# Edge layers of a graph network: target rows stored in edge order and loaded by plain DMA, index copies moved from GpSimd to ScalarE

## The chip, the cores and the metric

The kernel runs on one core of one Trainium2 chip. The metric is the device time of one execution in microseconds (us). Of the kernel before, three executions are shown, with their median.

## What is computed

Four graph layers run one after another on 100,000 nodes of 160 features (64 scalars and 32 vectors of three) and 25,000 edges, each with a source node `src` and a target node `dst`; the edges are sorted by `dst`. After each layer the new features are `layernorm(x + layer(x))`. The change touches the first three layers, which have this form (the third has no `alpha`, and a fixed factor in place of the count):

```python
y = linear(x)[src]                       # rows of the source nodes
w = mlp(edge_attributes)                 # one weight row for each edge
m = products of w, y and the 4 edge harmonics
s = segment_sum(m, dst)                  # by target node
x = layernorm(x + self_linear(x) * a + factor * (s @ W_out))
```

A target node's row needs four things: its own old row, the rows of its edges' sources, the sum over its run of edges, and its attribute `a`. Nodes that are no target of any edge are computed in a phase of their own, which the change leaves alone.

## The kernel before

The program is a row of phases: weights, all nodes without edges (to about 5,120 us of the span), the edge index, the three edge layers (5,148 to about 9,335 us), and then the attention layer in three phases. Each layer reads the node table of the layer before (`rows0`, `table1`, `table2`: rows of 164 floats, being features, mean, attribute and variance) and scatters the changed rows into the next one.

`edges_layer` (line 1071) does one edge layer; `l` is 0, 1 or 2 for the first, second and third. Edges go by 250 (two tiles of 125 partitions, `J` = 2) in four lanes (`LANES`), each lane with its own buffers and two PSUM banks. 25 rounds of four lanes make 100 *lane steps* for a layer. The order in which each engine issues its work is fixed by a table, `order` (line 1092): each step has a due time within a lane's round, and `staggered` (line 54) shifts the lanes by `part` = 10.70 and sorts. So within one lane step an engine does early steps of one lane and late steps of others. Each engine runs its list strictly in that order, and waits on counting semaphores. What follows touches these:

- GpSimd (POOL): `copy_keys` (line 1156), `roots` (line 1165, the powers of minus one half for the two rows of an edge; second and third layer only), `gather_next` with `gather` (lines 1140 to 1147), `scatter` (lines 1182 to 1190). An indirect DMA takes its row numbers from a small tile at a fixed address, so `gather` first copies four columns of row numbers into `ends_now` (line 1140), waits for that copy, and then issues four indirect DMAs (line 1147): source rows and target rows of each of two tiles. `scatter` does the same with `into_now` (line 1182) and two indirect DMAs (line 1190).
- VectorE (DVE): `root_attr` (lines 1223 and 1225), `normalize` (1236 and 1238), `mask` (1054 to 1056, reads `key_now`), products and factors, the new rows (1322, 1329), their statistics up to `widen` (1350, counted as `widened`), and the combinations of the messages (1269 to 1275, counted as `combined3`).
- ScalarE (ACT): `keep_attr` (1376) copies the target's attribute from the gathered row; the other steps copy PSUM results and activate.
- TensorE (PE): transposes (1436, 1448, 1450), matmuls, twelve filler matmuls per lane step (127), and the segment sums with the self term (1064 to 1068, 1494, 1496).
- SyncE (SP): three plain loads for each lane step (1123 to 1127).

`roots` of a lane waits for the rows gathered, DVE's `root_attr` waits for `roots`, `gather_next` waits for `normalize` (the buffer is then free), and `scatter` waits for `widened` of an earlier lane.

## Time and profile before

| | |
|---|---|
| Median of 3 runs | 12570.89 us (12570.47 to 12591.11) |
| The profiled execution's own time | 12567.56 us |
| Its span in the profile | 12565.9 us |
| Busy: PE, DVE, ACT, POOL | 9604.8, 8166.7, 4467.0, 5987.3 us |
| Granted TensorE clock, mean | 0.838 |
| The three edge layers, start of GpSimd's first and last instruction | 5147.9 and 9331.4 us |

Busy times are sums over instructions; an engine at 70% of the span may still be the one that sets the pace of a phase, so the phases are read one by one. POOL's DMA issues are counted busy (about 1.2 us each). In a timeline, the number in brackets is how long the engine was idle before the instruction, and what released it.

### The profile page before, as it was taken

How to read it: one execution, taken by the hardware profiler on the slowest of the kernel's cores; microseconds unless marked ns; L12 is line 12 of the kernel's file. 1: busy time of each engine (PE TensorE's matmuls, PEld its weight loads, DVE VectorE, ACT ScalarE, POOL GpSimd, SP SyncE). 2: the span in 40 equal slices, each digit the busy share in tenths (PEclk: the TensorE clock that was granted, in tenths of full speed). 3: DMA queues.
4: the chain of work that ended last, by engine and by line, in shares of the span. 5: the costliest groups of instructions: out<-in, count | busy, mean ns of one | idle time of the engine just before them, and what ended most of it. 6: DMA issues, size and time to landing. Idle time of an engine off the chain costs nothing. (4 is left out here: it accounts for less than half of the span.)

```text
span 12565.9 us, 239341 instructions
## 1 busy us (share of the span) xinstructions
PE 9604.8 (76%) x58771; PEld 8632.2 (69%) x58771; DVE 8166.7 (65%) x40535; ACT 4467.0 (36%) x16207; POOL 5987.3 (48%) x8005
## 2 busy tenths in 40 slices
PE   6777777777777777788868877788868788875998
PEld 5666666666666666677757776677757777765888
DVE  4555555555555555677756666566658888877777
ACT  3555555555555555322212221222212222221222
POOL 2333333333333333577756665666654444442444
PEclk8888878888888777899977787777778888888999
DMA  2222222222222222222211111211111111111111
GB/s 61 79 77 77 79 79 77 79 78 77 80 78 78 77 78 77 56 55 55 54 41 43 43 44 38 44 43 43 42 36 39 39 39 40 39 40 40 54 54 48
DMA packets 919772, 722.88 MB, mean 58 GB/s; under 512 B 453930, under 2 KB 871439, under 8 KB 919329
## 3 DMA queue, kind: packets, MB, share of 16 engines
q1 hardware_dynamic: 721696, 522.17, 14.8%
q0 software_dynamic: 197632, 196.80, 6.5%
q14 instruction: 410, 3.35, 0.1%
q8 instruction: 34, 0.56, 0.0%
HBM read 363.73 MB, written 360.00 MB: 58 GB/s over the span
## 5 line engine op out<-in xcount | busy, mean ns | idle before, releaser
L127 PE MATMUL bank<-ident 128*128 128x128 f32 x10000 | 1592.0, 313 | 97.2 <-PEq L883 59.3
L127 PEld LDWEIGHTS bank<-ident 128*128 128x128 f32 x10000 | 1539.6, 229 | 160.2 <-issue 60.0
L749 ACT ACTIVATE nodes_x<-nodes_z 125x161 f32<-125x161 f32 x2400 | 1006.5, 422 | 1515.6 <-DVE nodes_z L673 1515.4
L795 PE MATMUL bank<-ident,nodes_z 125*65 125x125 f32 x1600 | 496.6, 328 | 1216.2 <-DVE nodes_z L673 1215.9
L1147 POOL DMA_INDIRECT edge_rows<-table,edge_ends_now x832 | 1030.7, 1239 | 395.4 <-POOL edge_ends_now L1140 203.1
L795 PEld LDWEIGHTS bank<-ident,nodes_z 125*65 125x65 f32 x1600 | 262.0, 164 | 1294.4 <-issue 1293.9
L673 DVE SCALAR_TENSOR_TENSOR nodes_z<-bank,nodes_z 125x162 f32<-125x162 f32 x2400 | 812.3, 380 | 475.5 <-PE bank L814 451.0
L814 PE MATMUL bank<-self_v,nodes_v_t 128*125 128x98 f32 x4800 | 1079.0, 310 | 0.0
L663 DVE TENSOR_REDUCE nodes_sum<-nodes_z 125x2 f32<-125x322 f32 x400 | 195.2, 488 | 1298.6 <-DMA nodes_z<-rows 1298.3
L1190 POOL DMA_INDIRECT table<-edge_new,edge_into_now x600 | 742.0, 1237 | 486.0 <-issue 442.4
L812 PE MATMUL bank<-self_s,nodes_s_t 128*125 128x65 f32 x4800 | 931.2, 280 | 15.9 <-DVE ffn_y L233 13.7
L812 PEld LDWEIGHTS bank<-self_s,nodes_s_t 128*125 128x125 f32 x4800 | 870.3, 218 | 82.4 <-issue 38.0
L612 POOL TENSOR_SCALAR nodes_z<-nodes_sum 125x2 f32<-125x2 f32 x400 | 88.2, 220 | 1638.9 <-DVE nodes_sum L663 1638.9
L814 PEld LDWEIGHTS bank<-self_v,nodes_v_t 128*125 128x125 f32 x4800 | 808.9, 212 | 0.0
L627 POOL TENSOR_SCALAR nodes_x<-nodes_z,nodes_factor,nodes_offset 125x161 f32<-125x161 f32 x800 | 377.4, 482 | 764.5 <-DVE nodes_offset L692 764.5
L1739 POOL DMA_INDIRECT att_edge_rows<-table,att_edge_ends_now x416 | 511.8, 1230 | 194.1 <-POOL att_edge_ends_now L1732 98.9
L1223 DVE SCALAR_TENSOR_TENSOR edge_root_a<-edge_root,edge_rows 125x2 f32<-125x2 f32 x200 | 32.4, 162 | 878.5 <-POOL edge_root L1165 878.5
L1147 POOL DMA_INDIRECT edge_rows<-rows,edge_ends_now x416 | 506.0, 1216 | 195.9 <-POOL edge_ends_now L1140 99.7
L1408 ACT ACTIVATE edge_sums<-bank 125x163 f32<-125x163 f32 x600 | 151.2, 304 | 1235.9 <-PE bank L1496 1235.9
L271 POOL TENSOR_TENSOR ffn_root<-ffn_wide,half 125x4 f32<-125x4 f32 x400 | 403.1, 1008 | 327.9 <-DVE ffn_wide L198 327.9
L1273 DVE SCALAR_TENSOR_TENSOR edge_msg<-bank,edge_y,edge_msg 125x65 f32<-125x65 f32 x1800 | 509.8, 283 | 32.0
L1448 PE MATMUL bank<-ident,edge_xs 125*65 125x125 f32 x600 | 175.6, 314 | 447.1 <-DVE edge_xd L1238 434.3
(495 smaller groups left out, 31982.5 us busy)
## 6 DMA issues: line engine op xcount, KB each, us to landing
table<-nodes_z SPq DMA_DIRECT2D x1200, 160.2 KB
nodes_z<-rows SPq DMA_DIRECT2D x400, 160.2 KB
out<-nodes_res SPq DMA_DIRECT2D x400, 156.2 KB
nodes_v_t<-x_t SPq DMA_DIRECT2D x400, 94.7 KB
edge_dst_row<-dst SPq DMA_DIRECT2D x300, 122.1 KB
dest_rows<-kept SPq DMA_DIRECT2D x100, 316.4 KB
nodes_s_t<-x_t SPq DMA_DIRECT2D x400, 63.5 KB
kept<-att_keep SPq DMA_DIRECT2D x100, 218.8 KB
```

Source lines behind the costliest of these rows:

```text
L127: pe.matmul(banks[2 * ((n + lead) % LANES) + odd][:, 0:128], w["ident"][:, :], w["ident"][:, :], start=True, stop=True)
L271: p.tensor_tensor(f["root"][:, n, :], f["wide"][:, n, :], f["w"]["half"][:, 0:2 * J], ALU.pow).then_inc(t["pool"][n], 1)
L627: ins = p.tensor_scalar(x3[:, k, :], z[:, 3, k, 0:X], factor3[:, k:k + 1], offset3[:, k:k + 1], ALU.mult, ALU.add)
L673: ins = v.scalar_tensor_tensor(z[:, l + 1, k, 0:A + 1], banks[2 + n % 2][0:P, o:o + A + 1], z[:, l, k, A:A + 1], z[:, l, k, 0:A + 1], ALU. ...
L749: ins = act.activation(x3[:, k, :], z[:, l + 1, k, 0:X], ACT.Square, bias=z[:, l + 1, k, MEAN:MEAN + 1], scale=-1.0, accum_out=total[:, l, ...
L795: pe.transpose(banks[n % 2][0:S + 1, j * P:(j + 1) * P], z[:, l, k, 0:VS], ident)
L812: pe.matmul(banks[2 + n % 2][0:P, o:o + VS], xs[:, n, c], w[f"self_s{l}"][:, :], start=True, stop=True)
L814: ins = pe.matmul(banks[2 + n % 2][0:P, o + MEAN:o + A + 1], xv[:, n, c], w[f"self_v{l}"][:, :], start=False, stop=True, skip_group_check= ...
L1147: p.indirect_dma_start(e["rows"][:, n, side, j, :], None, source, bass.IndirectOffsetOnAxis(ap=e["ends_now"][:, side, k:k + 1], axis=0)).t ...
L1190: p.indirect_dma_start(target, bass.IndirectOffsetOnAxis(ap=e["into_now"][:, k:k + 1], axis=0), e["new"][:, n, j, :], None, bounds_check=n ...
L1273: v.scalar_tensor_tensor(scalars, bank[0:P, o:o + 1 + S], y, scalars, ALU.mult, ALU.add)
L1739: p.indirect_dma_start(e["rows"][:, n, side, j, :], None, table, bass.IndirectOffsetOnAxis(ap=e["ends_now"][:, side, k:k + 1], axis=0)).th ...
```

## The change

In the first and second layer, SP additionally stores the 250 new rows of each lane step in edge order, in a new DRAM tensor `ordered1` or `ordered2` (line `store_new`). In the second and third layer, SP loads those rows of the layer before with a plain DMA (`load_dst`) into the place of the target rows, and POOL gathers the source rows only. (Only the last edge of a target's run has that target's complete row; it is the only one whose result is scattered.) In all three layers the copies of keys, scatter numbers and gather numbers go from POOL to ACT's first step, `keep_attr`, one round ahead for the gather numbers; POOL's own copy is done once per layer for the first round. All due times but `load_dst`'s move back by 4.0, so that order among the old steps stays the same around the cycle.

```diff
+    sides = 1 if l else 2
+    per_gather = 16 * J * sides
+    ordered_view = [None if x is None else x.rearrange("(t p) f -> p t f", p=P) for x in ordered]
...
-              pool=["keys", *["roots"] * (l > 0)])
+              pool=["roots"] * (l > 0))
...
-             ("scatter", 33.1)]
+             ("scatter", 33.1), ("store_new", 33.1)]
+    order = [("load_dst", 0.0)] + [(step, begin + early) for step, begin in order]
...
+            def load_dst(n, i):
+                sp.wait_ge(t["dve"][n], count_at(t, i, "dve", "normed"))
+                gate(sp, t)
+                sp.wait_ge(t["act"][n], count_at(t, i, "act", "attr_kept"))
+                gate(sp, t)
+                sp.dma_start(e["rows"][:, n, 1, :, :], ordered_view[l][:, bass.ds(i * T + J * n, J), :]
+                             ).then_inc(dst_loaded[n], 16)
+
+            def store_new(n, i):
+                sp.wait_ge(t["dve"][n], count_at(t, i + 1, "dve", "widened"))
+                gate(sp, t)
+                sp.dma_start(ordered_view[l + 1][:, bass.ds(i * T + J * n, J), :], e["new"][:, n, :, :]
+                             ).then_inc(new_stored[n], 16)
...
-                p.tensor_copy(e["ends_now"][:, :, own], index["ends"][:, :, bass.ds(i * T + J * n, J)]
-                              ).then_inc(index_copied[n], 1)
-                p.wait_ge(index_copied[n], copies)
-                gate(p, t)
                 for j in range(J):
-                    for side in range(2):
+                    for side in range(sides):
...
-            def copy_keys(n, i):
...
             def roots(n, i):
-                p.wait_ge(gathered[n], 64 * i + 64)
+                p.wait_ge(gathered[n], per_gather * i + per_gather)
+                gate(p, t)
+                p.wait_ge(dst_loaded[n], 16 * i + 16)
                 gate(p, t)
...
             def scatter(n, i):
-                p.wait_ge(scattered[n], 16 * J * i + 16)
-                gate(p, t)
-                own = slice(J * n, J * n + J)
-                p.tensor_copy(e["into_now"][:, own], index["into_i"][:, bass.ds(i * T + J * n, J)]
-                              ).then_inc(index_copied[n], 1)
-                p.wait_ge(index_copied[n], 2 * i + 3)
+                p.wait_ge(t["act"][n], count_at(t, i + 1, "act", "attr_kept"))
                 gate(p, t)
                 p.wait_ge(t["dve"][n], count_at(t, i + 1, "dve", "widened"))
...
             def mask(n, i):
-                v.wait_ge(t["pool"][n], count_at(t, i + 1, "pool", "keys"))
+                v.wait_ge(t["act"][n], count_at(t, i + 1, "act", "attr_kept"))
...
             def keep_attr(n, i):
-                act.wait_ge(gathered[n], 64 * i + 64)
+                act.wait_ge(gathered[n], per_gather * i + per_gather)
+                gate(act, t)
                 act.wait_ge(scattered[n], 16 * J * i + 16)
+                gate(act, t)
+                if l:
+                    act.wait_ge(dst_loaded[n], 16 * i + 16)
+                    gate(act, t)
+                if l < 2:
+                    act.wait_ge(new_stored[n], 16 * i + 16)
+                    gate(act, t)
+                act.wait_ge(t["dve"][n], count_at(t, i, "dve", "masked"))
+                gate(act, t)
+                own, now = slice(J * n, J * n + J), bass.ds(i * T + J * n, J)
+                act.activation(e["key_now"][:, :, own], index["keys"][:, :, now], ACT.Copy)
+                act.activation(e["into_now"][:, own], index["into_i"][:, now], ACT.Copy)
+                act.activation(e["ends_now"][:, :, own], index["ends"][:, :, bass.ds(i * T + T + J * n, J)], ACT.Copy)
                 one(act.activation(e["new"][:, n, :, A:A + 1], e["rows"][:, n, 1, :, A:A + 1], ACT.Copy), n)
```

The change in POOL's list, in the body of the third layer's loop, one lane step before (in the names, `edge_` is the edge phase's prefix; `ISA` and `REGISTER_ALU` rows are address and wait work of the sequencer):

```order
L1165 TENSOR_TENSOR edge_root<-edge_rows,half 125x4
L1140 ISA
L1140 COPY edge_ends_now<-edge_ends 125x2x2
L1147 DMA edge_rows<-table,edge_ends_now 125x164 x4
L1182 ISA
L1182 COPY edge_into_now<-into_i 125x2
L1190 DMA table<-edge_new,edge_into_now 100000x164 x2
L1156 ISA
L1156 COPY edge_key_now<-edge_keys 125x2x2
L1165 TENSOR_TENSOR edge_root<-edge_rows,half 125x4
```

Between one `roots` and the next stand three copies and six indirect DMAs. With the change, two lane steps at the same place in POOL's list:

```order
L1171 DMA edge_rows<-table,edge_ends_now 125x164 x2
L1203 DMA table<-edge_new,edge_into_now 100000x164 x2
L1183 TENSOR_TENSOR edge_root<-edge_rows,half 125x4
L1171 DMA edge_rows<-table,edge_ends_now 125x164 x2
L1203 DMA table<-edge_new,edge_into_now 100000x164 x2
L1183 TENSOR_TENSOR edge_root<-edge_rows,half 125x4
```

Two of four gathers and the three copies are gone; the cycle roots, gather, scatter, roots is the same as before.

SP's list with the change, one lane step in the loop of the second layer:

```order
L1150 DMA ordered<-edge_new 125x2x164
L1144 ISA
L1144 DMA edge_rows<-ordered 125x2x164
L1130 ISA
L1130 DMA edge_attrs<-edge_attr 125x2x16
L1132 ISA
L1132 DMA edge_y<-edge_attr 125x2x4
L1134 ISA
L1134 DMA edge_dst_row<-dst 125x250
```

The store of one step's new rows stands ahead of the loads of the next round of the same lane, so these loads now wait behind `widened`.

ACT's list with the change, around its first step, in the second layer:

```order
L1417 ACTIVATE edge_dv_t<-bank 97x250
L1402 ISA
L1402 ACTIVATE edge_key_now<-edge_keys 125x2x2
L1403 REGISTER_ALU
L1403 ACTIVATE edge_into_now<-into_i 125x2
L1404 ISA
L1404 ACTIVATE edge_ends_now<-edge_ends 125x2x2
L1405 ACTIVATE edge_new<-edge_rows 125x2
L1382 REGISTER_ALU
L1431 ACTIVATE edge_f<-bank 128x250
```

The step has kept its place between the copy of the turned target rows and that of `linear`; three copies and their address work are added ahead of it.

## Rows read from the trace of the kernel before

**Rows 1.** Windows: length, busy us of PE, PEld, DVE, ACT, POOL; clock, DMA share, GB/s
```profile
5500.00:6000.00 500.00, 431.98 (x2924) 369.06 (x2923) 372.09 (x1761) 148.56 (x531) 350.79 (x400) 1.00 0.24 55
6600.00:7600.00 1000.00, 818.75 (x4416) 723.72 (x4416) 663.05 (x3105) 219.13 (x759) 636.32 (x690) 0.80 0.19 43
8100.00:9100.00 1000.00, 817.42 (x4436) 718.90 (x4435) 622.14 (x2835) 221.39 (x760) 634.63 (x694) 0.79 0.19 43
```
**Rows 2.** Timeline of POOL in the second layer (start, duration, instruction, idle before)
```profile
7019.21 0.41 POOL L1140 COPY edge_ends_now<-edge_ends 125x4 int32 x1 [1.84 <-DVE edge_xd L1238]
7020.61 1.29 POOL L1147 DMA_INDIRECT edge_rows<-table,edge_ends_now  x1 [0.99 <-POOL edge_ends_now L1140]
...
7025.32 1.21 POOL L1147 DMA_INDIRECT edge_rows<-table,edge_ends_now  x1 [0.30 <-issue]
...
7027.88 1.23 POOL L1190 DMA_INDIRECT table<-edge_new,edge_into_now  x1 [1.15 <-issue]
...
7030.62 0.21 POOL L1156 COPY edge_key_now<-edge_keys 125x4 f32 x1
7030.77 1.06 POOL L1165 TENSOR_TENSOR edge_root<-edge_rows,half 125x4 f32<-125x4 f32 x1
```
**Rows 3.** Timeline of DVE in the same lane step
```profile
7017.40 0.16 DVE L1223 SCALAR_TENSOR_TENSOR edge_root_a<-edge_root,edge_rows 125x2 f32<-125x2 f32 x1 [3.84 <-POOL edge_root L1165]
...
7023.97 0.16 DVE L1350 TENSOR_SCALAR edge_new<-edge_moments 125x2 f32<-125x2 f32 x1
...
7027.24 0.25 DVE L1275 SCALAR_TENSOR_TENSOR edge_msg<-bank,edge_y,edge_msg 125x32 f32<-125x32 f32 x1
7031.87 0.16 DVE L1223 SCALAR_TENSOR_TENSOR edge_root_a<-edge_root,edge_rows 125x2 f32<-125x2 f32 x1 [4.37 <-POOL edge_root L1165]
```
**Rows 4.** Timeline of DVE and POOL at the first layer's end
```profile
6310.06 0.16 DVE L1350 TENSOR_SCALAR edge_new<-edge_moments 125x2 f32<-125x2 f32 x1
...
6311.22 1.19 POOL L1190 DMA_INDIRECT table<-edge_new,edge_into_now  x1 [5.91 <-DVE edge_new L1350]
```
**Rows 5.** Third layer: timeline of DVE; line 1190 in window 8100:9100 (count, ns, starts)
```profile
8593.55 0.16 DVE L1223 SCALAR_TENSOR_TENSOR edge_root_a<-edge_root,edge_rows 125x2 f32<-125x2 f32 x1 [3.33 <-POOL edge_root L1165]
...
8599.32 0.23 DVE L1350 TENSOR_SCALAR edge_new<-edge_moments 125x2 f32<-125x2 f32 x1
...
L1190 POOL DMA_INDIRECT table<-edge_new,edge_into_now x140: 1212/1226/1242, 8098.9 to 9096.4; - x140
```
**Rows 6.** First layer: timeline of POOL; waits of PE in 5150:6290 (total, times, longest)
```profile
5600.67 1.38 POOL L1190 DMA_INDIRECT table<-edge_new,edge_into_now  x1 [1.15 <-issue]
...
5612.06 1.32 POOL L1190 DMA_INDIRECT table<-edge_new,edge_into_now  x1 [1.21 <-issue]
...
PE bank L1064 <- DVE edge_msg L1275: 101.2, 94, 1.2
```
**Rows 7.** Timeline of PE in the second layer, a lane step at the full clock
```profile
7019.01 0.29 PE L1448 MATMUL bank<-ident,edge_xs 125*65 125x125 f32 x1 [0.25 <-DVE edge_xd L1238]
...
7027.79 0.51 PE L1064 MATMUL bank<-edge_msg,edge_same 125*125 125x163 f32 x2 [1.53 <-DVE edge_msg L1275]
...
7029.85 0.41 PE L1496 MATMUL bank<-self_v,edge_dv_t 97*125 97x97 f32 x2
```
**Rows 8.** Timeline of ACT, the step after its first step
```profile
7023.48 0.38 ACT L1402 ACTIVATE edge_f<-bank 128x250 f32<-128x250 f32 x1 [1.65 <-PE bank L1467]
```
**Rows 9.** Timeline: plain loads issued, and the instruction that waited for them
```profile
6347.19 0.45 SPq L1127 DMA_DIRECT2D edge_dst_row<-dst  x1
...
6352.22 0.58 PE L1436 MATMUL bank<-ident,edge_attrs 125*16 125x125 f32 x2 [7.39 <-DMA edge_dst_row<-dst]
...
3002.74 2.10 SPq L582 DMA_DIRECT2D nodes_z<-rows  x1
...
3012.16 0.49 DVE L663 TENSOR_REDUCE nodes_sum<-nodes_z 125x2 f32<-125x322 f32 x1 [4.01 <-DMA nodes_z<-rows]
```
**Rows 10.** DMA queues of the page: packets, MB, share of 16 engines
```profile
q1 hardware_dynamic: 721696, 522.17, 14.8%
```

More of the change, by code:

```diff
@@ L1107, in edges_layer @@
     scattered = [sem(f"edges{l}_rows_scattered_lane{n}") for n in range(LANES)]
-    index_copied = [sem(f"edges{l}_index_copied_lane{n}") for n in range(LANES)]
+    dst_loaded = [sem(f"edges{l}_dst_rows_loaded_lane{n}") for n in range(LANES)]
+    new_stored = [sem(f"edges{l}_new_rows_stored_lane{n}") for n in range(LANES)]
+    first_ends = sem(f"edges{l}_first_ends_copied")
     ready = sem(f"edges{l}_ready")
@@ L1129, in load, with gather @@
                              ).then_inc(attrs_loaded[n], 16)
-            run_rounds(sp, rounds, order, part, dict(load=load))
+            def load_dst(n, i):
[10 more added lines that the diff above has]
+                             ).then_inc(new_stored[n], 16)
+            for n in range(LANES):
+                sp.sem_inc(new_stored[n], 16)
+            run_rounds(sp, rounds, order, part, dict(load=load, **(dict(load_dst=load_dst) if l else {}),
+                                                     **(dict(store_new=store_new) if l < 2 else {})))
+            if l < 2:
+                for n in range(LANES):
+                    sp.wait_ge(new_stored[n], 16 * rounds + 16)
         @block.gpsimd
         def _(p):
-            prime(p, t, "pool")
-            def gather(n, i, copies):
-                own = slice(J * n, J * n + J)
-                p.tensor_copy(e["ends_now"][:, :, own], index["ends"][:, :, bass.ds(i * T + J * n, J)]
-                              ).then_inc(index_copied[n], 1)
-                p.wait_ge(index_copied[n], copies)
-                gate(p, t)
+            if l:
+                prime(p, t, "pool")
+            def gather(n):
                 for j in range(J):
-                    for side in range(2):
+                    for side in range(sides):
                         k = J * n + j
@@ L1149, in gather, with roots @@
                                              ).then_inc(gathered[n], 16)
-            def copy_keys(n, i):
-                p.wait_ge(t["dve"][n], count_at(t, i, "dve", "masked"))
+            def roots(n, i):
+                p.wait_ge(gathered[n], per_gather * i + per_gather)
                 gate(p, t)
-                own = slice(J * n, J * n + J)
-                p.tensor_copy(e["key_now"][:, :, own], index["keys"][:, :, bass.ds(i * T + J * n, J)]
-                              ).then_inc(t["pool"][n], 1)
-            def roots(n, i):
-                p.wait_ge(gathered[n], 64 * i + 64)
+                p.wait_ge(dst_loaded[n], 16 * i + 16)
                 gate(p, t)
@@ L1174, in gather_next @@
                 gate(p, t)
[L1175 removed]
+                gather(n)
             def scatter(n, i):
[L1179 to L1184 removed]
+                p.wait_ge(t["act"][n], count_at(t, i + 1, "act", "attr_kept"))
                 gate(p, t)
@@ L1192, in scatter @@
                                          ).then_inc(scattered[n], 16)
+            p.tensor_copy(e["ends_now"][:, :, :], index["ends"][:, :, 0:T]).then_inc(first_ends, 1)
+            p.wait_ge(first_ends, 1)
             for n in range(LANES):
                 p.dma_start(e["first"][:, n:n + 1], inp["node_vec1"][0:P, :]).then_inc(scattered[n], 16)
-                gather(n, 0, 1)
-            run_rounds(p, rounds, order, part, dict(copy_keys=copy_keys, **(dict(roots=roots) if l else {}),
-                                                    gather_next=gather_next, scatter=scatter))
+                gather(n)
+            run_rounds(p, rounds, order, part, dict(**(dict(roots=roots) if l else {}), gather_next=gather_next,
+                                                    scatter=scatter))
             for n in range(LANES):
-                p.wait_ge(gathered[n], 64 * (rounds + 1))
+                p.wait_ge(gathered[n], per_gather * (rounds + 1))
                 p.wait_ge(scattered[n], 16 * J * rounds + 16)
@@ L2534, in program @@
     tables = [inp["rows0"]] + [nc.dram_tensor(f"table{l}", (nodes, ROW), F32).ap() for l in range(1, 4)]
+    ordered = [None] + [nc.dram_tensor(f"ordered{l}", (edges, ROW), F32).ap() for l in (1, 2)]
     kept = nc.dram_tensor("kept", (edges, KEPT), F32).ap()
@@ L2563, in program @@
                     sem, free = semaphores(nc)
-                    edges_layer(nc, sem, place(layer), banks, inp, w, e, index, tables, l, nodes, edges)
+                    edges_layer(nc, sem, place(layer), banks, inp, w, e, index, tables, ordered, l, nodes,
+                                edges)
                     free()
```

11 lines of the change are left out of this document (6 added, 5 removed).

## The prediction

> **What bounds the kernel now.** The change touches three phases of 100 lane steps each, so only these are read. First the windows, one in each edge layer: PE is busy 86, 82 and 82% of the time, DVE 74, 66 and 62%, POOL about 70, 64 and 63%, ACT 22 to 30% [rows 1]. No engine is full, so the pace must come from a chain of waits, which the timelines show. In the second layer DVE stands idle 3.84 and 4.37 us ahead of `root_attr`, each time until POOL's `roots` [rows 3]. POOL itself idles once in a step, 1.84 us, until DVE's `normalize` has freed the row buffer; the rest of its step is its own work: the copy of row numbers, 0.99 us until the first gather starts, four gathers to 7026.53, a copy and a 1.15 us gap, two scatters until 7030.62, the copy of keys and `roots` [rows 2]. So POOL's list plus one answer of DVE makes the step of 14.47 us (7017.40 to 7031.87). PE is not the bound: at the full clock one pass takes 11.25 us (7019.01 to 7030.26), 1.53 of it waiting, so 9.72 [rows 7]. The third layer steps by (9096.4 - 8098.9 - 1.5) / 69 = 14.43 us [rows 5]. In the first layer there is no `roots`, and POOL's list alone makes 11.39 us (5600.67 to 5612.06), while PE waits 1.08 us in a step for DVE, which waits for POOL's keys [rows 6].
>
> **What is removed.** In layers two and three POOL loses two gathers, 1.51 us each (0.30 gap and 1.21), the copy of row numbers (0.41, and a DMA that follows it starts 0.99 after it), the copy for the scatter (its start at 7026.53 to the scatter at 7027.88: 1.35, of which an ordinary 0.30 gap stays) and the keys (0.15 until `roots` starts) [rows 2]. That is 3.0 + 0.4 + 1.05 + 0.15 = 4.6 us of a step of 14.47. POOL alone would be at about 9.9. But POOL doesn't run alone, and the next wait in its list decides.
>
> **The wait that comes next.** POOL's scatter waits for `widened`, which before was long past: DVE reached it at 7024.13, and the scatter started at 7027.88 [rows 2, 3]. Now two gathers stand between. POOL took up work after `normalize` at 7019.21; even with 1.00 us from there to the first DMA they end by 7019.21 + 1.0 + 1.29 + 0.30 + 1.21 = 7023.0, ahead of `widened`. From here the step is a loop: `root_attr` to the end of `widened`, 7017.40 to 7024.13 = 6.73 us [rows 3]; from there to the start of the scatter; the two scatters, 7027.88 to 7030.62 = 2.74; `roots` until DVE starts, 7030.77 to 7031.87 = 1.10 [rows 2, 3]. The second term is not in the steady state of before. Its nearest rows are the layer's last scatters, where POOL did wait for `widened`: end of line 1350 at 6310.22, start of the DMA at 6311.22, 1.00 us [rows 4]. That agrees with the 0.99 that a gather needs after the copy it waits for [rows 2]. The lower bound is the 0.30 between DMAs that wait for nothing. I take 1.00, since it is the same wait at the same line.
> Second layer: 6.73 + 1.00 + 2.74 + 1.10 = **11.57 us**, against 14.47: 2.90 saved.
> Third layer: DVE's list is shorter there, 8593.55 to 8599.55 = 6.00 [rows 5], so 6.00 + 1.00 + 2.74 + 1.10 = **10.84**, against 14.43: 3.59 saved.
> DVE's own pass in the second layer is 7017.40 to 7027.49 = 10.09 us [rows 3], PE's 9.72 [rows 7]: both lie below the loop.
> First layer: POOL keeps four gathers; 5.8 us for them, 2.8 for the scatters, and at most 1.0 and 0.3 ahead of them make 9.9. DVE no longer waits for keys, so PE no longer waits for DVE: PE is the bound, at 11.39 - 1.08 = **10.31** [rows 6], 1.08 saved.
>
> **What is added.** *ACT*: three small copies; the nearest are POOL's, 0.2 to 0.4 us each [rows 2], with waits and addresses some 0.7 to 1.1 in all. They stand where ACT now idles 1.65 us until PE's `linear` [rows 8], so I cost them at nothing; without that cover each step of PE's would be later by their excess. DVE's `mask` now waits for this ACT step, due 6.4 units ahead of it: free. *SP*: `load_dst` and `store_new`, two DMAs of 164 KB in the second layer, one in each of the others. SP has nothing else that is urgent, but the loads of a lane's next round now queue behind `store_new`, which waits for `widened`. ACT's first step waits for both transfers, and behind it in ACT's list stand the copies that PE needs. When does it want them? PE turns the rows of a step 1.6 us after `root_attr` (7019.01), ACT's first step ends 2.8 us later (7023.48 - 1.65 = 7021.83) and so begins after 2.6 [rows 3, 7, 8], and `widened` is 6.73 after `root_attr`: 11.57 + 1.6 + 2.6 - 6.73 = 9.0 us after `widened`, or the step less 2.5. When do they land? Plain loads are bounded by a 122 KB load, issued with others at 6347.19 and used at 6352.22, 5.0 us, and a 160 KB load in the crowded node phase, 3002.74 to 3012.16, 9.4 us [rows 9]. The edge layers move 43 to 55 GB/s with a DMA share of 0.19 to 0.24 [rows 1], so I take 5 to 6 us: hidden, by 3 us. The end of a layer waits for the last stores, as it did for the last scatters.
> The trace says of the queue that a packet took 0.148 x 16 x 12565.9 / 721696 = 0.041 us on average [rows 10]. The Trainium skill (DMA: Bandwidth & Descriptors, on why a DMA increments its semaphore by 16) states that a plain DMA is spread over the largest number of engines up to 16 that divides its slowest dimension, so 125 partitions use five; no row here shows it. By it each new transfer, 250 runs, would hold five engines for 50 x 0.041 = 2.1 us, an estimate: 4.2 us of the second layer's 11.57, the sum unchanged, but two in series would eat most of the 3 us of slack. The case of late transfers below gets more chance for it.
> *Start of a layer*: eight gathers fewer ahead of the first `roots`, 8 x 1.51 = 12 us, in two layers 24.
>
> **The sum.** A layer has 100 steps, some 97 at the steady pace. 97 x 1.08 = 105; 97 x 2.90 = 281; 97 x 3.59 = 348; start 24. Together 758 us. The profiled execution took 12567.6, so 11810; the median of the runs is 3.3 above it, so **11813 us**, 6.0% less.
>
> **The rivals.**
> *PE's clock stays low.* In layers two and three, where the transposes wait behind DVE's 4 us for POOL, the mean granted clock was 0.80 and 0.79, a mix of its two levels; in the first layer, where PE waits about 1.1 us, it was 1.00, the full 2.4 GHz [rows 1, 3, 6]. In the loop PE waits about 0.4 us ahead of the transposes and 1.4 ahead of the sums, so I expect the level of the first layer. If it stays, PE needs 818.75 / 69.2 = 11.8 us a step [rows 1] plus 0.4 of waits, 12.2: 0.6 and 1.4 more in the two layers, 97 x 2.0 = 194, **12007**. Chance 0.12.
> *The scatter starts 0.3 us after `widened`.* Then 10.87 and 10.14, near DVE's and PE's passes: 97 x 1.4 = 136 less, **11677**. Against it stand rows 2 and 4. Chance 0.12.
> *Transfers a little late.* Store and load take 5 us each, one after the other, after 0.4 us of issue. ACT's first step wants them (step - 2.5) after `widened`, so the second layer steps at 10.4 + 2.5 = 12.9: 97 x 1.3 = 126 more, **11939**. Chance 0.12.
> *Slower: transfers late by much.* If each takes the node phase's 9.4 us and they follow one another, the second layer steps at 0.4 + 18.8 + 2.5 = 21.7 (7.2 more than before), the first, with a store only, at 12.3 (0.9 more), the third keeps its gain since no store precedes its load: 701 + 89 - 348 - 24 = 418 more than now, **12989**. It decides from about 8 us for each transfer. For it: ACT waits in order. Against it: in the node phase SP's issue itself was held up for 2.10 us, at the start of an edge layer it took 0.45 [rows 9]. Chance 0.04.
> That POOL's list is not shorter can be excluded: the order shows it.
>
> **How the numbers follow.** The forecast has 0.60. The range holds it with its neighbours, 11670 to 12020; outside are the late transfers by much and mixtures. 0.2% is 25 us, about what a measurement of this kernel can tell from no change; all cases but one lie hundreds below. Faster 0.94, same 0.02 (gain and late transfers near balance), slower 0.04.
>
> **What would show it.** Right: DVE's idle time ahead of `root_attr` falls from about 4 to 1.5 us and still ends with POOL; POOL's first scatter has a bracket that names DVE's line for `widened`, about 1.0 us after its end; the granted clock in layers two and three near 1.00; first layer near 10.3 us a step with no wait of DVE for keys; ACT's first step with no DMA as releaser. Wrong: a DMA of `ordered` named ahead of ACT's first step or of `roots`, PE busy at 0.8 of the clock, or the scatter following its gather without a wait.

## The result, and the profile after

The changed kernel took 11769.86 us (median of 3 runs, 11768.04 to 11792.64) against 12570.89: a ratio of 0.9363, 95% interval 0.9341 to 0.9386. The profiled execution took 11768.04, its span is 11766.3.

The unit of everything below is the **lane step**: one pass of the 250 edges of a lane. I measure it from the starts of a line that runs once in a step, ScalarE's copy of the turned attributes, as (last - first) / (count - 1). In the changed kernel that is line 1409 (count, shortest/mean/longest ns, first and last start), in a window of each layer:

```profile
L1409 ACT ACTIVATE edge_attr_t<-bank x50: 367/368/369, 5500.2 to 5996.1; 8x250 f32<-8x250 f32 x50
L1409 ACT ACTIVATE edge_attr_t<-bank x69: 367/368/369, 6505.6 to 7295.4; 16x250 f32<-16x250 f32 x69
L1409 ACT ACTIVATE edge_attr_t<-bank x73: 367/368/369, 7610.1 to 8389.8; 10x250 f32<-10x250 f32 x73
```

| us in a lane step | first layer | second | third |
|---|---|---|---|
| before | 11.32 | 14.50 | 14.44 |
| predicted | 10.31 | 11.57 | 10.84 |
| after | 10.12 | 11.61 | 10.83 |

The windows of the changed kernel answer to [rows 1]; columns as there:

```profile
5500.00:6000.00 500.00, 472.85 (x3262) 416.03 (x3261) 435.89 (x1977) 182.47 (x736) 360.46 (x297) 1.00 0.33 77
6500.00:7300.00 800.00, 642.74 (x4410) 557.85 (x4409) 657.63 (x3101) 238.62 (x964) 413.75 (x345) 1.00 0.28 68
7600.00:8400.00 800.00, 689.01 (x4729) 597.63 (x4728) 657.56 (x3028) 255.96 (x1035) 446.75 (x370) 1.00 0.26 57
```

The granted clock is 1.00 in all three, and no engine but PE in the first layer (472.85 of 500 us) is above 90%. The chain that carried the forecast stands in the timelines of the second layer, POOL and then DVE (start, duration, instruction, idle time before it and what ended it); they answer to [rows 2, 3]:

```profile
6903.37 1.06 POOL L1183 TENSOR_TENSOR edge_root<-edge_rows,half 125x4 f32<-125x4 f32 x1
6907.03 1.29 POOL L1171 DMA_INDIRECT edge_rows<-table,edge_ends_now  x1 [2.60 <-DVE edge_carry L1056]
6908.62 1.21 POOL L1171 DMA_INDIRECT edge_rows<-table,edge_ends_now  x1 [0.30 <-issue]
6912.24 1.22 POOL L1203 DMA_INDIRECT table<-edge_new,edge_into_now  x1 [2.41 <-issue]
6913.77 1.21 POOL L1203 DMA_INDIRECT table<-edge_new,edge_into_now  x1 [0.30 <-issue]
6914.99 1.05 POOL L1183 TENSOR_TENSOR edge_root<-edge_rows,half 125x4 f32<-125x4 f32 x1
...
6904.47 0.16 DVE L1238 SCALAR_TENSOR_TENSOR edge_root_a<-edge_root,edge_rows 125x2 f32<-125x2 f32 x1 [1.53 <-POOL edge_root L1183]
6911.03 0.16 DVE L1365 TENSOR_SCALAR edge_new<-edge_moments 125x2 f32<-125x2 f32 x1
6916.08 0.16 DVE L1238 SCALAR_TENSOR_TENSOR edge_root_a<-edge_root,edge_rows 125x2 f32<-125x2 f32 x1 [1.53 <-POOL edge_root L1183]
```

Follow it: `root_attr` at 6904.47, `widened` ends at 6911.19 (6.72 us), the scatter starts at 6912.24 (1.05), the two scatters take until 6914.99 (2.75), and 1.09 later DVE has `roots`. Together 11.61. The gathers ended at 6909.83, so POOL stands idle 2.41 us ahead of the scatter; the bracket says "issue", and it is the nearness to `widened` that names the cause (e1 tests it). The 1.05 us is not common to all that wait for `widened`: SP's store, which waits for the same instruction, started at 6911.47, 0.28 us after its end. ACT's first step:

```profile
6908.96 0.21 ACT L1402 ACTIVATE edge_key_now<-edge_keys 125x4 f32 x1 [0.16 <-issue]
6909.07 0.19 ACT L1403 ACTIVATE edge_into_now<-into_i 125x2 int32 x1
6909.16 0.19 ACT L1404 ACTIVATE edge_ends_now<-edge_ends 125x4 int32 x1
6909.26 0.19 ACT L1405 ACTIVATE edge_new<-edge_rows 125x2 f32<-125x2 f32 x1
6910.54 0.38 ACT L1431 ACTIVATE edge_f<-bank 128x250 f32<-128x250 f32 x1 [1.09 <-PE bank L1496]
```

No DMA releases it, and after its four small copies (6908.96 to 6909.45, 0.49 us in all, 0.30 of it for the three new ones) ACT is idle again for 1.09 us, where it was 1.65 [rows 8]: the copies are covered, and so were both transfers.

The 799.6 us of span divide as follows. A layer is taken from the start of GpSimd's first plain load (line 1196 before, 1211 after) to that of the next layer, the third to GpSimd's first copy of the attention layer. Saved are 6.7 us in the nodes before the edge layers, 127.6 in the first layer, 297.7 in the second and 369.7 in the third; all behind it took 2.1 us more, not less.

### The profile page after: what moved, and what is told of

Same layout as the page of the kernel before. It is cut to its first block and busy times, and to the rows that moved or that the text cites. A ratio compares the mean times of both kernels' runs of the same rounds, so it can differ in the third digit from the quotient of the medians.

```text
span 11766.3 us, 241538 instructions
## 1 busy us (share of the span) xinstructions
PE 9050.7 (77%) x58771; PEld 8149.1 (69%) x58771; DVE 8182.0 (70%) x40535; ACT 4552.9 (39%) x17107; POOL 5260.2 (45%) x6680
## 5 line engine op out<-in xcount | busy, mean ns | idle before, releaser
L127 PE MATMUL bank<-ident 128*128 128x128 f32 x10000 | 1477.6, 297 | 97.2 <-PEq L883 59.0
L127 PEld LDWEIGHTS bank<-ident 128*128 128x128 f32 x10000 | 1415.2, 213 | 145.8 <-issue 59.6
L1171 POOL DMA_INDIRECT edge_rows<-table,edge_ends_now x416 | 523.6, 1259 | 599.2 <-DVE edge_carry L1056 533.3
L796 PE MATMUL bank<-ident,nodes_z 125*97 125x125 f32 x1600 | 490.3, 324 | 0.0
L749 ACT ACTIVATION_READ_ACCUMULATOR nodes_x<-nodes_z 125x1 f32 x2400 | 454.4, 189 | 0.0
```

Source lines behind the costliest of these rows:

```text
L127: pe.matmul(banks[2 * ((n + lead) % LANES) + odd][:, 0:128], w["ident"][:, :], w["ident"][:, :], start=True, stop=True)
L749: ins = act.activation(x3[:, k, :], z[:, l + 1, k, 0:X], ACT.Square, bias=z[:, l + 1, k, MEAN:MEAN + 1], scale=-1.0, accum_out=total[:, l, ...
L796: ins = pe.transpose(banks[n % 2][0:V + 1, W + j * P:W + (j + 1) * P], z[:, l, k, MEAN:X], ident)
L1171: p.indirect_dma_start(e["rows"][:, n, side, j, :], None, source, bass.IndirectOffsetOnAxis(ap=e["ends_now"][:, side, k:k + 1], axis=0)).t ...
```

## The experiments

Eleven kernels were run, in four measurements with the kernel before in each; its median was 12600.75 (e1 to e4), 12571.73 (e5 to e7), 12572.27 (e8, e9) and 12596.86 us (e10, e11), so ratios compare better than times. The changed kernel was run again beside e5 to e7; it gave the same steps, and its ratio is the one to compare with:

> The changed kernel once more, on the chip of these experiments, for direct comparison: 10.12, 11.61 and 10.93 us a step in the three layers, and the ratio to the kernel before within the interval of the first measurement, 0.934 to 0.939.

Measured: 11784.15 us (11770.55 to 11806.23), ratio 0.9379 (0.9362 to 0.9395), steps 10.12, 11.62, 10.83. The phases that no experiment touches are less steady: the first edge layer began at 5139.6 us in this run and at 5207.6 in e4. So I compare lane steps first and totals second.

### Is the second and third layer's step the loop over the scatter?

**e1: the scatters behind the next lane's `roots`.**

```diff
-             ("scatter", 33.1), ("store_new", 33.1)]
+             ("scatter", 36.3), ("store_new", 33.1)]
```

> Edit to the changed kernel: the scatter's due time goes from 33.1 to 36.3, so GpSimd issues it behind the roots of the next lane step, not ahead of them; nothing else changes. Loop theory (the step of layers two and three is root_attr, widened, 1.0 us, two scatters, roots, root_attr): the scatters leave the loop, and what stays is VectorE's own pass, 10.1 us in layer two and 9.3 in layer three, with up to 0.4 us of waiting for the sums: steps of 10.4 and 9.8 us instead of 11.61 and 10.93, about 230 us less, 11540. The first layer has no roots and stays at 10.1. List theory (GpSimd's amount of work sets the step, wherever it stands): the list is as long as before, so 11.6 and 10.9, 11770.

Measured: steps 10.12, **10.52**, **9.72**; 11588.4 us (11553.35 to 11610.81), ratio 0.9199 (0.9178 to 0.9220). No instruction was removed. Timelines of POOL and DVE in the second layer:

```profile
6904.47 1.05 POOL L1183 TENSOR_TENSOR edge_root<-edge_rows,half 125x4 f32<-125x4 f32 x1
6906.91 1.26 POOL L1203 DMA_INDIRECT table<-edge_new,edge_into_now  x1 [1.39 <-issue]
6908.47 1.22 POOL L1203 DMA_INDIRECT table<-edge_new,edge_into_now  x1 [0.30 <-issue]
6911.97 1.23 POOL L1171 DMA_INDIRECT edge_rows<-table,edge_ends_now  x1 [2.28 <-DVE edge_carry L1056]
...
6905.68 0.16 DVE L1365 TENSOR_SCALAR edge_new<-edge_moments 125x2 f32<-125x2 f32 x1
6909.11 0.15 DVE L1238 SCALAR_TENSOR_TENSOR edge_root_a<-edge_root,edge_rows 125x2 f32<-125x2 f32 x1
```

The scatter again starts 1.07 us after `widened` ends (6905.84 to 6906.91), though it now stands behind `roots`, so it does wait for it; but `roots` is done by then, and `root_attr` has no bracket: DVE no longer waits for POOL. DVE is busy 568.82 of 600 us in a window (6500 to 7100), and the waits of that window name none of DVE's: its own pass is the bound. The loop theory holds; the theory that POOL's list sets the pace falls. This version beats both kernels: 97 steps by (1.09 + 1.11) are 213 us, and 0.0180 of 12590 (the difference of the ratios) are 227.

### Which half of the change brings what?

**e2: only the copies on ScalarE.** All rows are gathered again, with no plain load and no store. **e3: only the plain loads.** The three copies go back to POOL, with their waits; `mask` waits for POOL again.

```diff
-    sides = 1 if l else 2
+    sides = 2
```

```diff
-              pool=["roots"] * (l > 0))
+              pool=["keys", *["roots"] * (l > 0)])
...
+            def copy_keys(n, i):
...
-                act.activation(e["key_now"][:, :, own], index["keys"][:, :, now], ACT.Copy)
-                act.activation(e["into_now"][:, own], index["into_i"][:, now], ACT.Copy)
-                act.activation(e["ends_now"][:, :, own], index["ends"][:, :, bass.ds(i * T + T + J * n, J)], ACT.Copy)
```

> One half of the change alone: index copies on ScalarE as in the changed kernel, but target rows gathered by GpSimd in all layers, with no stores in edge order and no plain loads of them. Loop theory: in layers two and three the four gathers (5.9 us) now end behind widened, so the loop goes through them: normalize 1.46, 1.0 to the first gather, 5.9, 0.3, scatters 2.74, roots 1.1 make 12.5 us a step instead of 11.61 and 10.93. First layer 10.1 as in the changed kernel. Together 11770 + 97 x (0.9 + 1.6) + 24 = 12035. If ScalarE's copies gained nothing, layers two and three would be at 14.4 and the first at 11.4, as before.

> The other half alone: target rows by plain DMA in layers two and three as in the changed kernel, but all index copies on GpSimd, where they were before. First layer: 11.4 us a step, as before. Layers two and three: normalize 1.46, 1.75 until the first gather behind its copy, 2.8, the copy and its gap 1.35, scatters 2.74, keys and roots 1.25 make 11.35; in layer two the wait for widened (6.73 + 1.0) is a little later and gives 11.7, in layer three 11.35. So 11770 + 97 x (1.3 + 0.1 + 0.4) = 11945. By the amount of GpSimd's list (14.45 less two gathers) it would be 11.4 in both.

| | steps | time, ratio to before |
|---|---|---|
| e2, copies moved alone | 10.12 / 12.47 / 12.53 | 12104.77 us, 0.9607 (0.9586 to 0.9628) |
| e3, plain loads alone | 11.29 / 11.79 / 11.38 | 12035.82 us, 0.9554 (0.9531 to 0.9577) |
| both | 10.12 / 11.62 / 10.83 | 11784.15 us, 0.9379 (0.9362 to 0.9395) |

The steps came within about 0.1 us of what was expected. The totals came out 70 and 91 us above it, of which some 30 lie in this measurement (the kernel before took 12600.75 in it). The first layer's gain comes from the copies alone. In the second layer the parts save 2.03 and 2.71 us of a step, both together 2.89: they overlap, since once POOL's list is short enough the loop over `widened` stands, and a shorter list is worth nothing more. POOL in e3, second layer:

```profile
6953.45 0.34 POOL L1168 COPY edge_ends_now<-edge_ends 125x4 int32 x1 [1.91 <-DVE edge_xd L1268]
6954.77 1.30 POOL L1175 DMA_INDIRECT edge_rows<-table,edge_ends_now  x1 [0.98 <-POOL edge_ends_now L1168]
...
6957.68 0.19 POOL L1212 COPY edge_into_now<-into_i 125x2 int32 x1
6959.34 1.23 POOL L1220 DMA_INDIRECT table<-edge_new,edge_into_now  x1 [1.46 <-issue]
```

POOL copies the scatter numbers and is then idle for 1.46 us: with two gathers fewer ahead of it, that copy is hidden even on POOL. DVE's `widened` ended at 6958.29 in this step, 1.05 us before the scatter's start.

### Do the new transfers cost anything?

**e5: three stores for one.** Each store of new rows is followed by two more to spare tensors, and ACT's first step waits for all three.

```diff
+                for extra in ordered_spare[l]:
+                    sp.dma_start(extra[:, bass.ds(i * T + J * n, J), :], e["new"][:, n, :, :]
+                                 ).then_inc(new_stored[n], 16)
...
-                    act.wait_ge(new_stored[n], 16 * i + 16)
+                    act.wait_ge(new_stored[n], 48 * i + 16)
```

> In layers one and two each store of new rows in edge order is made three times (twice more into spare DRAM tensors that nobody reads), and ScalarE's first step waits for all three. My theory: transfers have about 3 us of slack, and two more of 2 us each in the same queue use that up and about 1 us more: layers one and two grow by 0 to 1.5 us a step (from 10.12 and 11.61), layer three stays at 10.93, total 11770 to 12050. If the transfers already were at their limit, each added one would cost its whole time, 2 us or more: 4 us a step in both layers, 12550. If the slack is larger than the two, nothing moves.

Measured: steps 10.12, 11.61, 10.83, unchanged; 11807.35 us, ratio 0.9394 (0.9378 to 0.9409). Windows of the first and second layer:

```profile
5500.00:6000.00 500.00, 473.01 (x3263) 416.06 (x3261) 434.56 (x1974) 184.06 (x739) 360.40 (x296) 1.00 0.47 110
6500.00:7300.00 800.00, 656.36 (x4411) 558.68 (x4410) 657.91 (x3099) 238.75 (x966) 412.79 (x345) 1.00 0.40 96
```

The DMA share went from 0.33 and 0.28 to 0.47 and 0.40, and the steps did not become longer. So a store, a load and two more stores fit into a step, and the two rivals with late transfers did not come true. But the slack is not as wide as the steady time suggests: a wait appeared that the changed kernel does not have. Waits in the second layer, 6500 to 7300 (total us, times, longest), where 69 steps were run:

```profile
ACT edge_key_now L1406 <- DMA table<-edge_new,edge_into_now: 68.7, 44, 2.0
ACT edge_key_now L1406 <- DMA edge_rows<-ordered: 31.3, 25, 1.6
```

In every step ACT's first step now waited for a DMA, by the profile for the scatters in 44 and for the plain load in 25, 1.45 us on average, and PE waited 28.8 us in all for SP's load of `dst`, which stands behind the stores. These waits filled time in which ACT and PE would have been idle. How much more traffic the step bears was not tried. The totals, 23 us apart, overlap in the intervals of their ratios.

### What do the filler matmuls do?

**e4: no fillers in the edge layers** (twelve matmuls a step whose result nobody uses).

```diff
-                **keep_busy(pe, banks, w, fill), turn_attr=turn_attr, turn_src=turn_rows("src", e["xs"]),
+                turn_attr=turn_attr, turn_src=turn_rows("src", e["xs"]),
```

> The twelve filler matmuls of each lane step are left out in the three edge layers (their results are used by nobody). They take 1.35 us of TensorE's 9.7 us. Loop theory: TensorE is no part of the loop in layers two and three, so with the clock still at 1.00 the steps stay at 11.6 and 10.9; if the granted clock falls for want of the fillers, TensorE's pass grows, and the steps grow where it passes the loop. First layer: if TensorE's pass is what sets 10.12 us, the step falls to about 9.8 (then the loop over the sums decides); if it stays at 10.12, TensorE was not the bound there.

Measured: steps 10.11, 11.94, 10.90; 11867.28 us, ratio 0.9410 (0.9390 to 0.9430).

```profile
5500.00:6000.00 500.00, 418.50 (x2671) 346.06 (x2670) 439.94 (x1981) 178.72 (x747) 364.05 (x297) 1.00 0.33 77
6500.00:7300.00 800.00, 623.41 (x3486) 519.55 (x3485) 650.33 (x3019) 224.03 (x938) 402.04 (x335) 0.90 0.28 66
```

Two things follow. In the second layer the clock fell to 0.90, a mix of its two levels, and the mean step grew by 0.33 although PE had less to do. The timelines show where: nearly all steps are either 11.62 or about 12.22 us long, by turns. In a long one (6511.50 to 6523.72) the sums matmuls ran at the lower level, 0.50 in windows of half a microsecond; those of the next step were at full clock again. PE, then DVE:

```profile
6510.34 0.88 PE L1064 MATMUL bank<-edge_msg,edge_same 125*125 125x163 f32 x2 [2.11 <-DVE edge_msg L1290]
6522.48 0.51 PE L1064 MATMUL bank<-edge_msg,edge_same 125*125 125x163 f32 x2 [1.44 <-DVE edge_msg L1290]
...
6515.04 0.28 DVE L1303 TENSOR_SCALAR edge_part<-edge_sums 125x2 f32<-125x2 f32 x1 [0.39 <-ACT edge_sums L1437]
```

The sums came late, DVE waited for them, and `widened` ended 7.32 us after `root_attr` in place of 6.72. The waits of the changed kernel's second layer name no wait of DVE for the sums; there PE is outside the loop. It enters it only when the clock is low.

And in the first layer PE lost 1.1 us of work a step at an unchanged clock, and the step did not move; PE now waited 0.6 us a step for DVE's combination (31.6 us, 49 times) and 0.6 for ACT (29.8, 49) where it had worked. **PE's list is not the first layer's bound**; the prediction had said that it was.

### What bounds the first layer?

The first reading was a loop over the sums: DVE's combination, PE's sums, ACT's copy, DVE's factor chain to `widened`, and the next combination. **e6** cuts it by putting the chain behind the next lane's combination (the steps between `limit_count` and `widen` are due at 35.65 to 36.9). **e7** is e6, and the fillers of the first layer are left out as well.

```diff
-             ("combine3", 24.85), ("add_up", 25.85), ("copy_sums", 28.7), ("limit_count", 29.4),
+             ("combine3", 24.85), ("add_up", 25.85), ("copy_sums", 28.7), ("limit_count", 35.60),
...
-             ("scatter", 33.1), ("store_new", 33.1)]
+             ("scatter", 37.0), ("store_new", 37.0)]
```

```diff
-                **keep_busy(pe, banks, w, fill), turn_attr=turn_attr, turn_src=turn_rows("src", e["xs"]),
+                **(keep_busy(pe, banks, w, fill) if l else {}), turn_attr=turn_attr, turn_src=turn_rows("src", e["xs"]),
```

> On the changed kernel: the due times of VectorE's chain from the factor to widened go back by some 6, so that it stands behind the combination of the next lane's messages and no longer between the sums and that combination; scatter and store follow it and so also stand behind the roots. Theory on the first layer: a loop of VectorE, TensorE and ScalarE sets its 10.12 us (end of combined3, sums on TensorE 2.8, their copy 0.5, then 6.8 us of VectorE from the factor to the next combined3). With the chain out of it VectorE waits for no sums and TensorE's pass decides, 9.6 busy and 0.4 waiting: 9.95. If TensorE's pass set the step already, it stays at 10.12. Layer two: VectorE's own list, 10.4 to 10.5 as with the scatter behind the roots; layer three 9.7. Total about 250 us below the changed kernel.

> As the kernel with the sums used later, and the twelve filler matmuls left out in the first layer alone, where the clock held at 1.00 without them in the run before. Theory: with the loop over the sums gone the first layer is bound by TensorE with the fillers (9.95) and by VectorE's list without them: 9.3 to 9.4 us a step, 50 us less in all. If the step doesn't fall below that of the kernel with the fillers, neither TensorE nor the loop was the bound there. Layers two and three as in that kernel.

Both missed. e6: steps **11.37**, 13.18, 12.47; 12231.05 us, ratio 0.9725 (0.9700 to 0.9750). e7: 11.92, 13.56, 12.46, with the clock at 0.93 in the first layer; 12273.78 us, 0.9755. Waits of e6 in 5500 to 6000 (total, times, longest):

```profile
ACT edge_key_now L1402 <- DMA table<-edge_new,edge_into_now: 134.3, 44, 4.1
...
DVE edge_msg L1284 <- PE bank L1513: 110.9, 44, 2.9
```

ACT's first step waits for the landing of the late scatters, 3 us a step, and copies for PE stand behind it. That looks like the cause. **e8** gives this step room: `keep_attr` is due at 4.5 in place of 0.0, behind `copy_attr`; this and e6's late chain in the first layer only, the others as e1. **e9** does both in all layers.

```diff
+    if l == 0:
+        late = dict(keep_attr=4.5, limit_count=35.60, invert=35.65, part_attr=35.70, half_factor=35.75,
+                    whole_factor=35.80, add_self=35.9, add_messages=36.1, measure=36.4, merge=36.7, widen=36.9,
+                    scatter=37.0, store_new=37.0)
```

```diff
-    if l == 0:
+    if True:
```

> Layers two and three as in e1 (scatters behind the next lane's roots), so 10.52 and 9.72 us a step there. In the first layer alone DVE's chain from limit_count to widened again stands behind the next lane's combine3, as in e6, but ScalarE's first step (keep_attr) is now due at 4.5 in place of 0.0, behind copy_attr, so that its wait for the scatters' landing has 4.5 units more. Theory 1: the first layer of the changed kernel is bound by the loop through the sums (10.12), and e6 lost there (11.37) only because ScalarE's first step stood 4.1 us in order behind the landing of the scatters. Then this step falls below 10.12, to about 9.5 to 9.8 (PE's busy time with its fillers is 472.85 / 49.4 = 9.6), and the total is 30 to 60 us below e1. Rival: the scatter's landing is not the cause of e6's loss, and something else that comes with the late chain (DVE's blocks of work in one piece, PE waiting for DVE) costs it; then the first layer stays at 11 or more, and the total is about 100 us above e1.

> The same two moves in all three layers. Theory 1 (landing of the scatters was what held ScalarE in e6): layers two and three leave e6's 13.18 and 12.47 for DVE's own pass, 10.5 and 9.7, as in e1; no DMA is named ahead of ScalarE's first step with more than about 1 us. Rival: in these layers gathers for the next round are also behind ScalarE's first step (gather_next waits for it), so the wait moves from ScalarE to POOL: the step stays at 11.5 or more, and POOL's roots are named as waiting for a gather's DMA.

Measured, e8: steps **11.43**, 10.50, 9.71; 11693.94 us, 0.9289 (0.9269 to 0.9310). e9: 11.43, 13.31, 12.44; 12239.16 us, 0.9729. Waits of e8 in the same window:

```profile
DVE edge_msg L1289 <- PE bank L1518: 113.4, 44, 4.1
...
ACT edge_key_now L1407 <- issue: 3.9, 11, 0.4
```

ACT's wait is gone and the step is what it was (11.37 in e6): theory 1 falls for this layer, the rival holds. The wait for the landing had only filled idle time. In e9 the second and third layer lost that wait too and stayed at e6's steps (13.18 and 12.47 there). That lies in what e9's rival said (11.5 or more), but not by the wait that it named: no wait of POOL's `roots` for a gather is on the list of the second layer (6700 to 7500), and DVE's wait for PE's messages is, with 176.3 us in 60 steps. What stayed is DVE's wait for PE's messages, and the timelines of DVE and PE in e8 show why:

```profile
5710.60 0.25 DVE L1295 SCALAR_TENSOR_TENSOR edge_msg<-bank,edge_y,edge_msg 125x32 f32<-125x32 f32 x1
5710.76 0.15 DVE L1327 TENSOR_TENSOR edge_part<-edge_sums,edge_new 125x2 f32<-125x2 f32 x1
...
5713.73 0.30 DVE L1261 TENSOR_SCALAR edge_xs<-edge_rows 125x161 f32<-125x161 f32 x1
...
5718.74 0.28 DVE L1289 TENSOR_SCALAR edge_msg<-bank,edge_y 125x65 f32<-125x65 f32 x1 [2.51 <-PE bank L1518]
...
5714.70 0.29 PE L1482 MATMUL bank<-ident,edge_xs 125*65 125x125 f32 x1 [0.99 <-DVE edge_xd L1262]
```

DVE works its list in order: combination, now the chain (5710.76 to 5713.73), then `normalize`. PE's transposes wait for `normalize`, and its messages of the *other* lane stand behind the transposes in PE's list; DVE's next combination waits for those. As these lines read, the chain had moved out of one loop into a longer one; no run tested that by itself.

That suggests how the changed kernel's own first layer runs. PE's timeline, then DVE's:

```profile
5704.01 0.52 PE L1064 MATMUL bank<-edge_msg,edge_same 125*125 125x163 f32 x2
5707.73 0.29 PE L1477 MATMUL bank<-ident,edge_xd 125*65 125x125 f32 x1 [0.39 <-ACT edge_v_t L1417]
5709.78 0.52 PE L1513 MATMUL bank<-edge_msg_d,edge_p 96*125 96x195 f32 x2
...
5707.05 0.16 DVE L1322 TENSOR_TENSOR edge_part<-edge_sums,edge_new 125x2 f32<-125x2 f32 x1 [0.75 <-ACT edge_sums L1437]
5710.34 0.29 DVE L1284 TENSOR_SCALAR edge_msg<-bank,edge_y 125x65 f32<-125x65 f32 x1 [0.21 <-PE bank L1513]
5713.56 0.25 DVE L1290 SCALAR_TENSOR_TENSOR edge_msg<-bank,edge_y,edge_msg 125x32 f32<-125x32 f32 x1
```

Sums matmuls, transposes and messages on PE, 5704.01 to 5710.30; DVE's combination 5710.34 to 5713.81; back to the sums matmuls at about 5714.1: 10.1 us. The path over the sums is 0.21 shorter, since DVE is through with the chain that much before the messages come. The fillers stand outside this loop, behind the messages, which is why e4 changed nothing. **e10** lengthens the sums path of the changed kernel, **e11**, made on e1, shortens the message path.

```diff
+                for j in range(J):
+                    act.activation(e["again"][:, n, j, 0:M], banks[2 * n + j][0:P, 0:M], ACT.Copy)
                 for j in range(J):
                     ins = act.activation(e["sums"][:, n, j, 0:M], banks[2 * n + j][0:P, 0:M], ACT.Copy)
```

```diff
-             ("messages", 20.3), ("combine0", 22.2), ("combine1", 23.15), ("combine2", 24.0),
+             ("messages", 20.3 if l else 19.3), ("combine0", 22.2), ("combine1", 23.15), ("combine2", 24.0),
```

> The changed kernel, but ScalarE copies the sums of a step twice, first to a spare tile, so that the real copy ends about 0.5 us later (its two copies take 0.50 in the trace). ScalarE itself is busy 36% and has room. In the first layer three readings differ. (a) PE's own list is the bound: nothing changes, 10.12. (b) The loop over the sums (combination on DVE, sums on PE, copy on ScalarE, factor chain on DVE, next combination) is the bound: 10.12 + 0.5 = 10.6. (c) The loop runs over PE's messages: sums matmuls, transposes and messages on PE 6.3 us, then DVE's combination 3.4 and 0.4 back to PE, 10.1; the path over the sums is shorter by the 0.2 us that DVE waits for the messages (0.21 ahead of line 1284): 10.12 + 0.5 - 0.2 = 10.4. I hold (c). In layers two and three widened comes up to 0.5 us later where DVE waits for the sums, so 11.61 and 10.83 rise by 0 to 0.5.

> e1 (scatters behind the roots) and in the first layer PE's messages matmuls due at 19.3 in place of 20.3, which puts them ahead of turn_dst and hidden2 on PE's list; layers two and three as in e1 (10.52, 9.72). By (c) of e10 the loop over the messages shortens by about 1.4 us and the sums path is next: 10.12 - 0.2 = 9.9 us in the first layer, 20 us less than e1 in all. By (b), the sums alone, and by (a), PE's list, it stays at 10.12. A rival for worse: turn_dst and hidden2 come 1.3 us later, so that ScalarE's copies and then PE's linear are late, and the first layer goes to 10.5 or more.

e10: steps **10.47**, 11.62, 10.82; 11870.64 us, 0.9425 (0.9410 to 0.9439). (a) falls: PE got no work and the step grew. Between (b), 10.6, and (c), 10.4, the run is nearer to (c) but does not separate them cleanly, since the extra copies also delay ACT's copies of the turned rows, which lie in the message path:

```profile
PE bank L1479 <- ACT edge_v_t L1417: 35.5, 48, 0.7
DVE edge_msg L1284 <- PE bank L1515: 4.2, 27, 0.2
```

PE waits 0.74 us a step there, 0.39 before, and 0.35 is just what the step grew. DVE still waits for the messages in 27 of 48 steps: the two paths have become about equal.

e11: steps **10.05**, 10.61, 9.72; 11589.38 us, 0.9203 (0.9188 to 0.9218), the same as e1 in the total. DVE no longer waits for the messages at all, as (c) says, but the gain is 0.07 and not 0.2, for a new wait takes over (waits in the first layer's window):

```profile
DVE edge_part L1322 <- ACT edge_sums L1437: 44.7, 50, 1.0
...
PE bank L1495 <- ACT edge_h L1427: 32.7, 50, 0.7
```

With the messages ahead, ACT's activation for `linear` is late and PE stands 0.65 us; its own list, 9.4 us (467.25 us of 49.8 steps), plus this is the 10.05. So, as far as these runs show, the first layer sits where three paths are nearly equal, over the messages (10.12), over the sums (9.9) and PE's list (9.6 with its waits left out). The one move that helped, e11, was worth 0.07 us.

## Why the prediction was right, and where it was not

- **The wait that comes next.** The step that carried most of the sum was the loop `root_attr`, `widened`, scatter, `roots`, with 6.73 + 1.00 + 2.74 + 1.10 = 11.57. Measured: 6.72 + 1.05 + 2.75 + 1.09 = 11.61; the third layer 10.83 against 10.84. The one term that was not in the steady state of before, the start of a scatter that waits, was taken from [rows 4] as 1.00 and is 1.05; the rival with 0.3 (11677 us) is refuted by the same timeline, and e1 shows that the loop and not POOL's list decides.
- **The first layer.** "PE is the bound, at 11.39 - 1.08 = 10.31" failed in its mechanism: e4 took 1.1 us of PE's work away without effect. It is a loop over PE's sums, transposes and messages and DVE's combination; e10 and e11 moved it as that loop says in sign, not exactly in size, and how much each of the near-equal paths holds it stays open. As a term it was undersized: 1.08 x 97 = 105 us forecast; the steps gave 97 x (11.32 - 10.12) = 116, and the whole phase 127.6. The 11.39 came from one lane step; the mean of the window was 11.32. The subtraction took PE's waits for DVE out of the step as if PE's other work were unbroken; that 10.31 came within 2% of 10.12 was luck: three paths lie within 0.5 us there, and PE's list happens to be one of them.
- **Starts of a layer.** 24 us for two layers were taken. The phases saved 297.7 and 369.7, of which the steady part is 97 x 2.89 = 280 and 97 x 3.61 = 350, so 17 and 20 came from starts and ends, 37 and not 24. With 23 more than forecast in the first layer and 7 in the node phase, which the change does not touch, and 2 lost behind the layers, that makes the 42 us between 758 and 799.6.
- **The clock.** Forecast 1.00 in layers two and three, against 0.80 and 0.79 before [rows 1]; measured 1.00. The reason given, shorter waits of PE, agrees with e2, e6 and e7, whose second layers have longer steps (12.47, 13.18, 13.56) and 0.92, 0.86 and 0.81, and with e4, where the fillers were missing (0.90). No run changed PE's waits alone.
- **Additions costed at nothing.** ACT's copies take 0.49 us with the old one and not 0.7 to 1.1, and are hidden. The transfers are hidden; e5 tripled the stores. The Trainium skill's rule on the number of engines (DMA: Bandwidth & Descriptors, on why a DMA increments its semaphore by 16) had given the late-transfer rival its chance; no run counts the engines that a transfer uses, but whatever their number, two more stores in every step cost no time, so the rule decided nothing here.
- **The slower side.** Its mechanism, ACT's first step in order behind a transfer, did occur: in e6 and e7 for late scatters (in e6's first layer up to 4.1 us, ahead of line 1402), and in e5 in each of the 69 steps read of the second layer (up to 2.0 us). In e5 it did not set the step, which was unchanged, nor in e6, as e8 and e9 showed; for e7 no run tells.

## What to carry to other kernels

When an engine's list gets shorter, look at what its remaining waits hold up: the new step is the longest loop through several in-order lists, and each term of it can be read from the trace of before if a place is found where that wait already happened (here a layer's last scatter). Then ask whether something in the loop needs to be there: moving two scatters behind `roots` by one due time added about a quarter to what the whole change had brought. And a wait that a view names with a large total may merely fill idle time: give it room by itself, as e8 did, before calling it the cause.

## What was not expected of the hardware

- An indirect DMA that waits for a semaphore started 1.05 and 1.07 us after the instruction that it waited for had ended (after, e1), 0.98 after a copy on its own engine (e3); one that waits for nothing follows at 0.30. SP's plain store, waiting for the same instruction as the scatter, started after 0.28 (after).
- The granted clock answered to fillers in one layer and not in another: without them it stayed at 1.00 in the first layer and fell to 0.90 in the second. There it did so by turns: the sums matmuls of about every second step ran at the lower level, and those steps took 12.22 us and the others 11.62.
- Phases that no edit touches moved by up to 68 us between profiled executions (start of the first edge layer 5139.6 to 5207.6); the prediction had called 25 us the limit of the measurement. Lane steps told apart what totals could not: the first layer's was 10.12 in each of after, its second run, e1, e2 and e5. They are not exact to the last digit everywhere: the second layer's was 10.52, 10.50 and 10.61 in e1, e8 and e11, where it is the same program, and 13.18 and 13.56 in e6 and e7, again the same program there, with the clock at 0.86 and 0.81.
